# Rows of a table of integers in SBUF that begin at a multiple of 16 bytes

## What is computed

```python
x = _layernorm(x + gated(x, edge_attr_64))        # messages with gates, mean over the edges of a node
x = _layernorm(x + sage_mean(x))                  # feat @ W_self + mean of neighbours @ W_neigh
x = _layernorm(x + gat(gat(x, edge_attr_128)))    # two attention layers: weighted sum over the edges
x = _layernorm(x + sage(sage(x)))                 # two more mean layers, each with a norm and a relu
```

## Time and profile before

| | |
|---|---|
| profiled execution | 2015.3 us |
| its span (first to last instruction) | 2013.4 us |
| TensorE matmul busy | 1737.6 us (86%) |
| TensorE weight load busy | 1404.0 us (70%) |
| VectorE busy | 1410.2 us (70%) |
| ScalarE busy | 912.9 us (45%) |
| GpSimd busy | 983.9 us (49%) |

### The profile page before, as it was taken

The page is one execution under the profiler, slowest core; times in us unless marked ns, Lnnn a source line. Parts: engine busy times, 40 slices in busy tenths (PEclk is TensorE's granted clock), DMA queues, the critical chain, the costliest instruction groups (busy, mean ns, idle before and its releaser), DMA issues. The chain is left out here.

```text
span 2013.4 us, 43000 instructions
## 1 busy us (share of the span) xinstructions
PE 1737.6 (86%) x13651; PEld 1404.0 (70%) x13651; DVE 1410.2 (70%) x4286; ACT 912.9 (45%) x2490; POOL 983.9 (49%) x998
## 2 busy tenths in 40 slices
PE   6699999999998748998558999957699999299996
PEld 5699999999998615556446888746478778166664
DVE  4678888888887788995667676555776664644656
ACT  2566676667676366663304454421244443411100
POOL 3767677777775200000457777726677774300000
PEclk9799999999999859999659999976699999699998
DMA  6988788888886002222452111117121111345442
GB/s 191 258 248 235 238 246 245 255 253 252 239 253 198 12 1 98 112 121 110 148 114 62 44 41 42 48 30 215 43 65 42 42 42 34 124 164 198 186 164 88
DMA packets 149675, 276.87 MB, mean 138 GB/s; under 512 B 28807, under 2 KB 88845, under 8 KB 147188
## 3 DMA queue, kind: packets, MB, share of 16 engines
q1 hardware_dynamic: 109134, 191.58, 29.5%
q0 software_dynamic: 35456, 79.88, 14.0%
q10 hardware_dynamic: 4854, 2.55, 0.5%
HBM read 228.82 MB, written 45.08 MB: 136 GB/s over the span
## 5 line engine op out<-in xcount | busy, mean ns | idle before, releaser
L961 POOL DMA_INDIRECT gated_rows<-p_tab,src_idx x416 | 429.5, 1033 | 177.2 <-issue 105.6
L1353 POOL DMA_INDIRECT ring<-table,src_idx x384 | 384.9, 1002 | 144.2 <-issue 91.4
L2164 PE MATMUL bank<-counts,mean_xs 128*128 128x416 bf16 (+2 forms) x1350 | 219.1, 321 | 32.6 <-DVE mean_xs L1673 32.6
L1002 PE MATMUL bank<-gated_wide_q,gated_comb 128*128 128x256 f32 x832 | 216.2, 383 | 0.0
L1159 DVE TENSOR_TENSOR gated_pre<-bank,gated_rows 128x512 f32<-128x512 f32 x208 | 142.8, 687 | 101.8 <-PE bank L1002 101.8
L1484 ACT COPY attention_counts<-bank 128x475 f32 (+1 forms) x224 | 127.4, 569 | 177.3 <-PE bank L1508 154.6
L2164 PEld LDWEIGHTS bank<-counts,mean_xs 128*128 128x128 bf16 x1350 | 126.0, 97 | 116.6 <-issue 34.7
L1519 PEld LDWEIGHTS bank<-attention_counts,h_sb 128*128 128x128 f32 x900 | 157.5, 190 | 62.6 <-ACT attention_counts L1484 4.0
L1075 ACT ACTIVATE gated_sig<-gated_pre 128x512 f32<-128x512 f32 x208 | 131.1, 630 | 153.4 <-DVE gated_pre L1159 151.4
L1519 PE MATMUL bank<-attention_counts,h_sb 128*128 128x232 f32 (+1 forms) x900 | 191.9, 341 | 2.5 <-DVE attention_counts L1576 2.0
L1508 PE MATMUL bank<-attention_wide_b,scratch 128*128 128x400 f32 x448 | 189.1, 504 | 0.0
(11 more groups left out here) (428 smaller groups left out, 4001.2 us busy)
## 6 DMA issues: line engine op xcount, KB each, us to landing
counts<-count_tabs SPq DMA_DIRECT2D x16, 2675.0 KB, 9.8
h_sb<-in_edge_attr_dram SPq DMA_DIRECT2D x51, 512.0 KB
count_tabs<-mean_counts SPq DMA_DIRECT2D x40, 535.0 KB, 2.7
gated_relr<-rel_rows SPq DMA_DIRECT2D x104, 128.0 KB
gated_ids<-id_rows SPq DMA_DIRECT2D x26, 512.0 KB
gated_wide_q<-q_tab SPq DMA_DIRECT2D x208, 64.0 KB
attend_hot_lo<-low_hots SPq DMA_DIRECT2D x52, 256.0 KB, 3.9
gated_ea<-in_edge_attr_dram SPq DMA_DIRECT2D x51, 256.0 KB
```

The lines of the kernel that those rows point to most:

```text
L961: pool.indirect_dma_start(out=rows[:, q % TICKS, c, :], out_offset=None, in_=p_tab, in_offset=bass.IndirectOffsetOnAxis(ap=src_idx[:, b, j ...
L1002: mm = pe.matmul(PRE[q % 2][:, c * 2 * P:(c + 1) * 2 * P], comb[:, u, k, c, :], wide_q[:, u, c, :], start=True, stop=True)
L1353: pool.indirect_dma_start(out=rows[:, n % RING, j, :], out_offset=None, in_=table, in_offset=bass.IndirectOffsetOnAxis(ap=src_idx[:, gathe ...
L2164: mm = pe.matmul(BANKS_D[q % ND][:, 0:width], xs[l][:, m // 3, m % 3, :], counts[:, s % 2, m // 3, at:at + width], start=(m == 0), stop=(m ...
```

## The change

The table's rows are padded. Each block gets 28 integers (112 bytes) for its 26, or 16 (64 bytes) for its 14, so that each begins at a multiple of 16 bytes. `place_m` grows from 208 to 224 integers, `place_a` from 112 to 128. The cast that fills a table writes eight rows with a gap between them, and the three places that read take the row's new start. How many integers are read, and when, stays.

```diff
-    place_m, origin_m = sb("place_m", [1, NB * PAIRS], I32), sb("origin_m", [1, LAST], I32)
-    place_a, origin_a = sb("place_a", [1, NSB * ATP], I32), sb("origin_a", [1, LAST], I32)
+    MROW, AROW = [-(-used // 4) * 4 for used in (SBP, ATP)]
+    place_m, origin_m = sb("place_m", [1, NSB * MROW], I32), sb("origin_m", [1, LAST], I32)
+    place_a, origin_a = sb("place_a", [1, NSB * AROW], I32), sb("origin_a", [1, LAST], I32)
...
-                        link(pool.tensor_copy(places[:, :], place_f[:, here]))
+                        link(pool.tensor_copy(places.rearrange("a (s c) -> a s c", c=line)[:, :, 0:used], at_f))
...
-                                values = loaded_starts(mybir.EngineType.Activation, place_a[0:1, n:n + ATP], A_COLS - WP)
+                                values = loaded_starts(mybir.EngineType.Activation, place_a[0:1, n // ATP * AROW:n // ATP * AROW + ATP], A_COLS - WP)
...
-                            values = loaded_starts(mybir.EngineType.DVE, place_a[0:1, n:n + ATP], A_COLS - WP)
+                            values = loaded_starts(mybir.EngineType.DVE, place_a[0:1, n // ATP * AROW:n // ATP * AROW + ATP], A_COLS - WP)
...
-                            values = loaded_starts(mybir.EngineType.Activation, place_m[0:1, n:n + SBP], M_COLS - WP)
+                            values = loaded_starts(mybir.EngineType.Activation, place_m[0:1, n // SBP * MROW:n // SBP * MROW + SBP], M_COLS - WP)
```

More of the change, by code:

```diff
@@ L399, in _ @@
                     heads = first_row.rearrange("a (s c) -> a s c", c=2 * SBP)[:, :, 0:2 * SBP:2]
-                    for kind, (blocks, used, origins, places) in enumerate(((M_BLOCKS, SBP, origin_m, place_m), (A_BLOCKS, ATP, origin_a, place_a))):
+                    for kind, (blocks, used, line, origins, places) in enumerate(((M_BLOCKS, SBP, MROW, origin_m, place_m), (A_BLOCKS, ATP, AROW, origin_a, place_a))):
                         here = slice(sum(FAR[0:kind]), sum(FAR[0:kind + 1]))
```

## The result

| | before | after |
|---|---|---|
| median of the runs, us | 2013.57 (4 runs, 2007.76 to 2017.7) | 1998.78 (4 runs, 1997.75 to 2001.66) |
| ratio, 95% interval | | 0.9926 [0.9902, 0.9949] |
| profiled execution, us | 2015.3 | 1998.6 |
| its span, us | 2013.4 | 1996.8 |
| mean granted clock | 0.915 | 0.914 |

The forecast was a ratio of 0.9923 and 15.5 us; the medians lie 14.8 us apart, the profiled executions 16.7. The kernel is faster, and by the forecast amount.

What follows compares the result with a forecast made beforehand. ScalarE's slow reads were taken to bound the mean build's odd blocks, GpSimd's gathers the attention passes. Gains of 8.3 + 3.7 + 3.45 = 15.5 us took the 2012.5 us median to 1997.0, range 1990 to 2006.

Steps and rivals of the forecast that it cites:

- The reads: Line 757: slow odd-row reads of `place_m` go from 5.56 to 1.94 us, 14.5 us of ScalarE in all.
- Rival C: Nothing happens: address isn't the cause, or each register has its price anywhere; time stays 2012.5 us; chance 0.04.
- Blocks 3 and 5: Mean build: these odd blocks become like blocks 4 and 6, 22.25 us on average, gaining 8.3 us together.
- both full: Mean build, even blocks 4 and 6 (22.4 and 22.1 us): VectorE busy 22.3 of 22.4 us, TensorE 22.0.
- Block 7: Mean build's last block: TensorE's 1.99 us pause and 1.7 us lost to the clock go, 3.7 us.
- Block 1: Mean build, block with the self terms: TensorE's 3.45 us standstill behind the read goes; an earlier clock rise counted as nothing.
- 1.7 us that I named as an upper bound: Mean build, block 1: the clock might come up sooner, up to 1.7 us more, left out of the forecast.
- Attention: Attention passes: gains in blocks 1, 3 and 5 are given back in block 6; 0, bounds 0 to 4.6 us.
- Rival B: Attention pays too, up to 4.6 us more, plus 1.7 from block 1's clock; 1990.7 us; chance 0.07.
- Padding: Prologue: GpSimd's two casts take 0 to 1 us more, hidden by its idle time; moved allocations count 0.
- rival A: Mean build: VectorE takes the place of the read, so the gain is 11.3 us; 2001.2 us; chance 0.13.
- D: After the mean build: TensorE's clock granted less often, sixteen falls making it slower, 2024.2 us; chance 0.04.

Runs made afterwards that it cites:

- odd_off: The changed kernel with the same table sizes and strides, but odd rows set 8 bytes further in, off a multiple of 16; 2014.91 us, 1.0004.
- stride27: The changed kernel with rows 27 and 15 integers apart, so that starts are 0, 12, 8 and 4 bytes off in turn; 2023.92 us, 1.0046.
- three_reads: The kernel before, unpadded, with ScalarE reading a mean-build block's 26 integers in three parts (8, 9 and 9); 2012.91 us, 0.9984.
- full_quads: The changed kernel with the padding read too, 28 registers for 26 and 16 for 14, the table cleared first; 2000.00 us, 0.9922.
- before_clear_pool: The kernel before with the mean build's clears of the next count table moved from ScalarE to GpSimd; 2012.38 us, 0.9974.
- block1_off: The changed kernel with one `place_m` row, block 1's, starting 8 bytes off; 2003.24 us, 0.9948.
- a_only: The kernel before with only `place_a`, the table of the attention passes, padded; 2017.04 us, 1.0015.
- aux_last: The changed kernel with the 25 small gathers of each attention pass issued behind the last gather of rows; 1988.35 us, 0.9874.
- before_aux_last: The kernel before with the 25 small gathers of each attention pass issued behind the last gather of rows; 2008.56 us, 0.9967.
- all_three: The changed kernel with whole rows read, the small gathers last and the clears on GpSimd; 1989.63 us, 0.9857.
- quads_aux_last: The changed kernel with whole rows read (28 and 16 integers) and the small gathers last; 1989.55 us, 0.9866.

## Why the prediction was right, and where it wasn't

*The reads.* As forecast, all at 1.92 to 1.94 us, and for the reason given: `odd_off` and `stride27` show the address as the cause. Rival C is out. The Trainium skill (Runtime: NRT & Kernel Launch, Instruction fetch mechanics) puts a register load at about 200 ns per register, even in bulk; the page speaks of loads from HBM, and these read SBUF. For starts off 16 bytes this case comes to the same figure (5.55 / 26 = 0.213 us); for starts on it the figure doesn't hold here (1.93 / 26 = 0.074).

*Blocks 3 and 5: 8.3 us forecast, 7.7 measured.* The step "they become like even blocks" held. The reason that I gave for the excess over 3.62 us did not: I put it down to the clock. In the earlier trace rows block 5 is 26.2 us long at a clock of 1.00, and it lost 3.6 us, the bare difference of the reads; only block 3's 0.94 has the clock in it, and block 3 lost 0.5 us more, not the 1.6 of the prediction. The reading that TensorE is held up just by what exceeds its four banks fell with `three_reads`.

The reading that the even blocks are set by VectorE and TensorE, "both full", fell too. ScalarE, busy for 16.7 of 22.4 us, has no room either: in blocks 4 to 6 of before and of after, 24 of the 26 steps from copy to copy are 0.74 to 0.80 us, 0.77 on average, and the two longer ones are the read's (2.15 us, 5.81 when slow) and the clear's (1.84, 1.56 in block 6). 24 x 0.77 + 2.15 + 1.84 = 22.5 us and 24 x 0.77 + 5.81 + 1.84 = 26.1, measured 22.4 and 26.2: ScalarE's chain sets an even block as well as an odd one, and what the read takes less, the block does. That the blocks of `full_quads` follow the read by another 0.2 us fits it. TensorE is close behind: with the clear taken off ScalarE the even blocks of `before_clear_pool` fell only to 21.7 us, TensorE busy for all of it.

As a sum over several blocks: ScalarE, when it is behind, starts a copy about every 0.75 us at best, while TensorE starts a pair every 0.85 (order of time in block 3 of after, first ScalarE, then TensorE):

```profile
817.23 0.58 ACT L1788 CAST mean_counts<-bank 128x500 f32 x1 [0.16 <-PE bank L1841]
817.98 0.62 ACT L1788 CAST mean_counts<-bank 128x500 f32 x1 [0.16 <-ACT mean_counts L1788]
...
803.82 0.19 PE L1838 MATMUL bank<-mean_onto,mean_lo 128*128 128x25 bf16 x1
804.67 0.18 PE L1838 MATMUL bank<-mean_onto,mean_lo 128*128 128x25 bf16 x1
```

So ScalarE wins back 0.1 us a pair, 2.6 a block, and in the blocks above it never quite catches up. Against that, each block adds its read's idle (5.24 slow, 1.54 fast) and a clear (1.4). Over two blocks: before 5.24 + 1.54 + 2.8 - 5.2 = 4.4 us too much, after 2 x 1.54 + 2.8 - 5.2 = 0.7. On TensorE's pace of 22.1 us a block (26 x 0.85) that gives 48.6 and 44.9 us; measured 48.3 to 49.0 and 44.7 to 45.0. For `three_reads`, with 8.5 us of idle around its six reads, the same sum gives 50.3 us, measured 49.9 to 50.2. It is fitted to the runs, and holds only where ScalarE's chain is the longest: in `before_clear_pool` it would give 46 us and 48.0 were measured, because there TensorE, with its pause and a fall of the clock in each odd block, takes longer than ScalarE.

*Block 7: 3.7 forecast, 3.9 measured.* Pause and clock both gone; the stretch shows 1.00 for all of the block.

*Block 1: 3.45 forecast, 6.0 measured, the mis-sized term.* The pause was right, "the clock there is at 0.5 already, I give that nothing" was not: without the pause TensorE comes up to 2.4 GHz 8 us earlier. The 1.7 us that I named as an upper bound was drawn from a fall in block 7, where the clock was down for 3.4 us (the 0.42 and 0.26 that it lacked of 2.5 us each are half of that), and was too small too. `block1_off` puts the same read at 4.3 us; over the kernels with a slow one the term is 4.3 to 6.6.

*Attention: 0 forecast.* About right on the total (+0.9 and +0.2 us in the profile, `a_only` 1.0015), and the cause is shown by `aux_last` against `before_aux_last`: with GpSimd out of the way, the same alignment is worth 2.9 us. I expected no loss and put the lower bound at 0; a loss of about 1 us a pass is there over all kernels, though no single trace shows it clear of scatter. Block 6 takes 36.0 to 38.3 us with the padded table, 34.8 to 36.1 without, and 33.9 and 32.9 in `stride27`, the slowest reader: it takes back what the blocks before it gained, and somewhat more. Why more is open; in after it is a clock of 0.95. Rival B's money exists, but is locked behind the gathers. The wait in block 6 did not grow by what was gained: 3.6 us before and after. TensorE's busy time there grew instead, from 32.38 us to 34.12, at the lower clock.

*Padding: 0 forecast.* Nothing of it is to be seen; it lies in the first stage, whose length scatters by more.

*The rivals A and D.* After, VectorE is busy for all of blocks 3 to 6, which looks like rival A come true. But the blocks are 22.1 to 22.6 us long, not 23.5, and ScalarE's chain accounts for that. Rival A's case came only with `all_three`, where the blocks are 23.0 us and ScalarE has room. And busy is no bound: the same masks took longer in `quads_aux_last`, first here, than in after, second, in blocks of the same length or shorter (ns, shortest, median and longest):

```profile
L1900 DVE TENSOR_SCALAR mean_wide_b<-code_iota,code x106: 324/367/401, 800.1 to 889.9; 128x400 bf16<-128x400 f16 x106
```

```profile
L1900 DVE TENSOR_SCALAR mean_wide_b<-code_iota,code x106: 304/314/345, 799.9 to 889.8; 128x400 bf16<-128x400 f16 x106
```

D didn't happen, though its mechanism is there: after has two falls of the clock in the passes, one each, where before has none. It needed sixteen.

The total came out right in part because errors cancelled: block 1 gave 2.5 us more, blocks 3, 5 and 0 together 1.1 less, the passes and the stage between them took back 3.7, the first stage and the others gave 3.2.

## What to carry to other kernels

Let every table that an engine reads into registers start its rows at multiples of 16 bytes and, where the padding is harmless, read whole groups of four: with 26 registers that is 1.9 instead of 5.6 us (1.7 for 28), during which the engine takes up nothing. What it brings depends on the stage: where that engine feeds the bound one, a read costs about its whole length, even if every single stop is shorter than the buffers are deep, because an engine without holes has nothing to pay it back with. Whether it has holes is read from the steps between its instructions, not from its busy share, which was 75% on ScalarE. Where something else is late, it brings nothing until that is moved (here it even cost about 1 us a pass), in this kernel 25 small gathers a pass, which cost 7 us in all in the middle of before's stream and 10 in after's. A trace in which the same instruction on the same data has two durations holds the experiment already: sort it by address before building anything.

## What the runs showed of the hardware that was not expected

- A start 4, 8 or 12 bytes off costs the same (5.54 to 5.59 us for 26 registers), 0.21 us for each register; 28 aligned registers take less time than 26 (1.73 and 1.93 us).
- Cutting a read in three parts of 0.56 to 2.80 us left the stage 13 us longer than one aligned read did, though no part is as long as the work in the four banks.
- A register read in the middle of a block took up to 2.80 us where the same count from the same kind of address took 1.97 in blocks 0 and 1; the reason is open.
- Beside a GpSimd memset of 1.7 us one VectorE mask took 1.12 us instead of 0.28, and the blocks were 0.7 us longer (89.0 to 91.7 us for four).
- VectorE's masks had a median of 314 ns in one kernel and 367 in another with the same code, with no block longer for it. A duration in a trace can hold waiting of its own.
